# A graph layer that gathers every tile of edge rows on POOL, with no rows fetched one by one, and counts every fourth gather

## The chip, the cores and the metric

The kernel runs on one core of one Trainium2 chip. The metric is the time of one execution on the device in microseconds (us). The median of three runs of the kernel before is 1577.52 us (1574.93 to 1591.05 us).

The engines are named as the profile names them: PE is TensorE (PEld is its loading of weights), DVE is VectorE, ACT is ScalarE, POOL is GpSimd, SP is SyncE. A "q" behind a name (SPq, ACTq) means the engine's sequencer, which issues DMAs, loads registers and waits.

## The reference, cut to what matters

There are 6250 nodes with 128 features, 106250 edges sorted by destination, and 40 relation types.

```python
S   = segment_sum(x[src], dst * 40 + edge_type)          # (6250, 40, 128)
cnt = segment_sum(ones,   dst * 40 + edge_type)          # (6250, 40)
agg = einsum('nrd,rdf->nf', S, relation_weights) + cnt @ rFeatures
h   = agg * deg ** -0.5                                  # deg: edges per destination, at least 1
h   = relu(h + h @ loop_weight)
out = layernorm(x + h, axis=-1)
```

The costly part is `x[src]`: one row of 128 features for each of the 106250 edges, read in an order that the data give, and its sum into (destination, relation) cells.

## The kernel before, in words

**Tiles and blocks.** The edges are cut into 831 tiles of 128 edges (the last has 10). Seventeen tiles make a block (`TPB`), and a block of tiles belongs roughly to 128 destination nodes. There are 49 blocks; `i` is the block, `k` the place of a tile in it, and t = 17 i + k the tile.

**What a tile goes through.** (1) The 128 rows of the tile's sources are brought from DRAM into SBUF. From tile 51 on they come from `x_parts`, a copy of x in which each row is 1 KB: a high part and a low part, whose sum is the fp32 value. The first 51 tiles are gathered from x itself into `raw` and split by ACT and DVE. (2) DVE makes a one-hot matrix of 128 edges by 480 cells (`one_hot`, L896), 40 relations times a window of 12 nodes. (3) PE multiplies (L1148, two matmuls of 480 columns, one for each part) into one of six PSUM banks; a small matmul for each tile (L1130) counts the edges. (4) ACT copies 11 of the 12 window columns from PSUM to `ring` (L692) and (5) DVE adds the first column to what is there (L1028). Then the bank is free again. Between the tiles PE also multiplies the finished block before with the 40 relation weights (`relations`, L1160), and the nodes of the block before that are finished (layer norm and store).

**How rows come in.** There are three ways.

- POOL gathers a whole tile by one indirect DMA (`gather`, L572; L579 for the first 51). A gather writes `rows[:, k]`, so tile t needs tile t - 17 to be done: POOL waits for `tile_done` (L571), which PE raises by two after every odd `k` and by one after k = 16.
- The 19 tiles of `BY_ROW` (18 tiles from block 6 on, 41 tiles apart as a rule, and the last one with 10 rows) are fetched by SP, one DMA of 1 KB for each row: 18 times 128 and 10, that is 2314 DMAs. SP loads 32 row addresses into registers at a time (L523) and then issues 32 DMAs (L526). Six tiles can be held in `by_row`; before tile j SP waits until tile j - 6 of its list is done (L519).
- The 5 tiles of `BY_ACT` are fetched in the same way by ACT, one row after each copy (`fetch`, called at L694, DMA at L669): 640 DMAs.

PE waits before L1148 for the tile's own rows: `by_row_landed`, `by_act_landed` or `gathered` (L1132 to L1138).

**The count of gathers.** Each gather also raises `gather_issued` when its descriptors are written (`engine_sem`), 807 times in all. DVE waits for it before each add (L1026 and L1027): at tile t the gather of tile t + 17 - t // 4 must be issued, and from tile 48 on that of tile t + 5. Nothing else reads this count.

**Order at the start.** SP loads edges and x, issues 19 small loads of the row numbers for its list (L496 to L498), then the load of the window positions (L500), for which ACT and DVE wait, and then stores the parts of x (L476). DVE turns row numbers into byte addresses (L1051 and L1053) before its main loop. POOL gathers tiles 0 to 50 from x beside this. Gathers from `x_parts` begin when all of it is stored.

Of the kernel before, what the change touches and what calls it, by code (L numbers as in the profile page):

```python
# [14 lines left out]
P = 128  # L15
# [7 lines left out]
TPB = 17  # L23
# [15 lines left out]
ROW_LOAD = 32  # L39
# [10 lines left out]
SAFE = 6  # L50
SUMS_FROM = 10
# [20 lines left out]
ROW_TILE = 6  # L72
BY_ROW = [(6 + j * 41 // 17) * TPB + ROW_TILE for j in range(18)] + [-(-E // P) - 1]
BY_ROW_BUFS = 6
ACT_FROM = 4
ACT_ROWS = 1
ACT_BLOCKS = 8
ACT_TILE = 12
BY_ACT = [i * TPB + ACT_TILE for i in [*range(ACT_FROM + ACT_BLOCKS, BLOCKS - 1, ACT_BLOCKS)]]
ACT_BUFS = 2  # L80
ACT_LOAD = 4
ROW_BYTES = 2 * D * 4
# [23 lines left out]
assert ACT_ROWS * ACT_BLOCKS * TPB >= P and P % ACT_LOAD == 0 and BY_ACT[-1] < FULL and not set(BY_ACT) & set(BY_ROW)  # L106
# [26 lines left out]
def build(nc, x, src_main, src_by_tile, src_rest, dst_main, dst_rest, type_main, type_rest, r_features, relation_w, loop_w, out):  # L133
    with ExitStack() as ctx:
# [65 lines left out]
        by_row = x_out.rearrange("p h n c d -> p (h n) c d")  # L200
        by_act = by_row[:, BY_ROW_BUFS:BY_ROW_BUFS + ACT_BUFS]
        act_src = sb("act_src", [len(BY_ACT), P], I32)
        act_at = sb("act_at", [len(BY_ACT), P], I32)
        by_row_src = sb("by_row_src", [len(BY_ROW), P], I32)
        by_row_at = sb("by_row_at", [len(BY_ROW), P], I32)
        x_bytes = x_parts.bitcast(U8).rearrange("n b -> (n b)").unsqueeze(0)
# [82 lines left out]
        by_row_cleared = sem("by_row_cleared")  # L289
        by_row_src_loaded = sem("by_row_src_loaded")  # L290
        by_row_ready = sem("by_row_ready")
        act_src_loaded = sem("act_src_loaded")
        act_ready = sem("act_ready")
        by_act_landed = [sem(f"by_act_landed{j}") for j in range(len(BY_ACT))]
        by_row_landed = [sem(f"by_row_landed{j}") for j in range(len(BY_ROW))]
# [56 lines left out]
        def gathers_through(t):  # L352

            return t + 1 - len([n for n in BY_ROW + BY_ACT if n <= t])
# [94 lines left out]
        def _(sp):  # L449
# [6 lines left out]
            sp.dma_start(act_src[:], src_by_tile[BY_ACT[0]:BY_ACT[-1] + 1:ACT_BLOCKS * TPB, :]).then_inc(act_src_loaded, 16)  # L456
# [49 lines left out]
            def in_order():  # L506
# [6 lines left out]
                sp.wait_ge(src_loaded, 2 * 16)  # L513
                for b in range(STAGE_BUFS):
                    sp.wait_ge(staged[b], stage_count(b) * 16)
                sp.wait_ge(by_row_ready, 1)
                for j, t in enumerate(BY_ROW):
                    if j >= BY_ROW_BUFS:
                        sp.wait_ge(tile_done, BY_ROW[j - BY_ROW_BUFS] + 1)  # L519
                    for first in range(0, rows_in_tile(t), ROW_LOAD):  # L520
                        ps = range(first, min(first + ROW_LOAD, rows_in_tile(t)))
                        index = [sp.alloc_register(f"sp_row{j}_{p}") for p in ps]
                        sp.load(index, by_row_at[j:j + 1, ps[0]:ps[-1] + 1])  # L523
                        for p, reg in zip(ps, index):
# [781 lines left out]
```

## Time and profile before

| what | value |
|---|---|
| median of the runs | 1577.52 us (1574.93 to 1591.05) |
| span of the profiled execution | 1576.6 us |
| PE busy | 1049.6 us (67%) |
| DVE busy | 732.7 us (46%) |
| POOL busy | 798.1 us (51%), 756 gathers from `x_parts` and 51 from x |
| ACT busy | 528.4 us (34%) |
| DMA packets | 71124, 127.58 MB, 81 GB/s on average |
| mean granted TensorE clock | 0.853 of full speed |

The profile shows one execution, whose own time is its span of 1576.6 us, 0.9 us below the median. "Busy" leaves out what sequencers do, so SP, which only issues, has no busy time at all. Waits are listed as "engine, its line <- what ended the wait: us in total, times, longest". "issue" means that nothing in the profile explains the wait, and "remote" that a semaphore's update was seen to which no instruction's end belongs.

### The profile page before, as it was taken

Reading aid. Unit: us, or ns where it says so; the run is one execution under the profiler, and the core shown is the slowest. Engines: PE = TensorE matmul, PEld = TensorE weight load, DVE = VectorE, ACT = ScalarE, POOL = GpSimd, SP = SyncE. Lnnn points to the kernel's source line nnn. Section 1 sums busy time; section 2 is a strip of 40 time slices with the busy share of each in tenths; the row PEclk is TensorE's granted clock in tenths of the full one; section 3 lists DMA queues with packets and bytes.
Section 4 is the critical chain, followed back from the end, with each engine's and each line's share of the span. In section 5 each row is a group of like instructions: output and inputs, shape, how many; then the busy total and the mean of one; then the engine's idle time right before and its main releaser. Section 6 shows DMA issues by size and latency. Waiting matters only on the chain.

```text
span 1576.6 us, 31507 instructions
## 1 busy us (share of the span) xinstructions
PE 1049.6 (67%) x6713; PEld 931.1 (59%) x6713; DVE 732.7 (46%) x2573; ACT 528.4 (34%) x1119; POOL 798.1 (51%) x822
## 2 busy tenths in 40 slices
PE   1388777847774768474687486746576657774868
PEld 0277667736763668464576375635565546664758
DVE  5464555525452545243455254534354525552545
ACT  2353333323332334232343133323243313331433
POOL 7536565626562556353555264636364635562650
PEclk9989998969796888687998798968798979877989
DMA  6623332313231323131333132313132312231320
GB/s 200 215 62 89 90 92 77 93 45 91 77 91 46 87 78 88 48 91 44 88 87 89 45 84 70 95 46 89 54 88 70 91 51 83 82 88 46 86 77 22
DMA packets 71124, 127.58 MB, mean 81 GB/s; under 512 B 18417, under 2 KB 44002, under 8 KB 70930
## 3 DMA queue, kind: packets, MB, share of 16 engines
q0 software_dynamic: 37920, 102.48, 22.9%
q1 hardware_dynamic: 17698, 16.04, 3.3%
q10 hardware_dynamic: 15312, 7.01, 1.6%
q8 instruction: 56, 0.92, 0.3%
q14 instruction: 138, 1.13, 0.2%
HBM read 115.86 MB, written 9.60 MB: 80 GB/s over the span
## 4 chain that ended last, share of the span: by engine, by line
SPq 58%; issue 33%; PE 3%; DMA 0%; DVE 0%; ACT 0%; DVEq 0%; ACTq 0%
SPq L526 50%; SPq L523 8%; PE agg_ps L1160 1%; PE win_ps L1148 1%; PE win_ps L1233 1%; DMA x_parts<-x_out 0%; DMA x_out<-x_parts 0%; PE win_ps L1186 0%; ACT ring L692 0%; PE win_ps L1130 0%; PE win_ps L1237 0%; PE win_ps L1185 0%; DVE h_sb L935 0%; DVE y_sb L939 0%; DVE y_mid L945 0%
## 5 line engine op out<-in xcount | busy, mean ns | idle before, releaser
L572 POOL DMA_INDIRECT rows<-x_parts,src x756 | 745.8, 986 | 717.9 <-PE win_ps L1148 414.4
L692 ACT COPY ring<-win_ps 128x451 f32 x831 | 465.4, 560 | 948.5 <-PE win_ps L1148 420.1
L1160 PEld LDWEIGHTS agg_ps<-ring,w 128*128 128x128 f32 x3936 | 619.6, 210 | 106.4 <-issue 56.5
L1160 PE MATMUL agg_ps<-ring,w 128*128 128x128 f32 x3936 | 629.8, 294 | 45.0 <-issue 44.1
L1148 PE MATMUL win_ps<-hot,rows 128*128 128x480 f32 x1614 | 595.9, 457 | 12.3 <-issue 10.0
L1028 DVE TENSOR_TENSOR ring<-ring,win_ps 128x41 f32 x831 | 187.1, 225 | 808.2 <-ACT ring L692 606.2
L896 DVE TENSOR_SCALAR hot<-iota,key_f 128x480 fp32r<-128x480 f16 x831 | 393.7, 474 | 3.7 <-issue 3.7
L1148 PEld LDWEIGHTS win_ps<-hot,rows 128*128 128x128 f32 x1614 | 271.6, 210 | 14.7 <-issue 10.2
L1130 PE MATMUL win_ps<-hot_node,hot_type 128*128 128x12 bf16 x831 | 87.3, 172 | 214.9 <-DVE ring L1028 109.9
L1130 PEld LDWEIGHTS win_ps<-hot_node,hot_type 128*128 128x128 bf16 x831 | 70.9, 103 | 262.1 <-issue 215.1
L1148 PE MATMUL win_ps<-hot,x_out 128*128 128x480 f32 x48 | 24.1, 597 | 230.2 <-DMA x_out<-x_parts 227.4
L1148 PEld LDWEIGHTS win_ps<-hot,x_out 128*128 128x128 f32 x48 | 10.4, 270 | 231.8 <-DMA x_out<-x_parts 228.8
L579 POOL DMA_INDIRECT raw<-x,src x51 | 50.5, 991 | 22.6 <-issue 17.8
L916 DVE TENSOR_TENSOR hot_type<-iota,typ_f 128x320 bf16<-128x320 f16 x98 | 49.6, 506 | 0.0
L964 DVE TENSOR_TENSOR ring<-ring 128x492 f32<-128x492 f32 x48 | 31.8, 662 | 0.0
L975 DVE COPY ring<-zeros 128x492 f32<-128x492 f32 x47 | 30.8, 656 | 0.0
L990 DVE COPY ring<-zeros 128x492 f32<-128x492 f32 x47 | 30.3, 645 | 0.0
L1186 PE MATMUL win_ps<-loop,agg_sb 128*128 128x128 f32 x96 | 23.6, 323 | 3.8 <-issue 3.8
L909 DVE TENSOR_TENSOR hot_node<-iota,rel_f 128x96 bf16<-128x96 f16 x98 | 25.3, 258 | 0.4 <-issue 0.4
L1185 PEld LDWEIGHTS win_ps<-ones,cnt_sb 128*128 128x128 f32 x96 | 18.5, 194 | 3.5 <-issue 0.7
L641 ACT CAST rows<-raw 128x256 fp32r<-128x256 f32 (+1 forms) x27 | 10.4, 394 | 22.0 <-remote 18.7
L1186 PEld LDWEIGHTS win_ps<-loop,agg_sb 128*128 128x128 f32 x96 | 15.2, 197 | 4.0 <-issue 4.0
(94 smaller groups left out, 259.7 us busy)
## 6 DMA issues: line engine op xcount, KB each, us to landing
x_out<-x_parts SPq DMA_DIRECT2D x2314, 1.0 KB
rows<-x_parts,src POOLq DMA_INDIRECT x756
x_out<-x_parts ACTq DMA_DIRECT2D x640, 1.0 KB
x_parts<-x_out SPq DMA_DIRECT2D x6, 512.0 KB
x_parts<-ring SPq DMA_DIRECT2D x6, 512.0 KB
out<-out_sb ACTq DMA_DIRECT2D x48, 64.0 KB
x_blk<-x ACTq DMA_DIRECT2D x47, 64.0 KB
w<-relation_w SPq DMA_DIRECT2D x8, 320.0 KB
```

The source lines that it names most:

```text
L523: sp.load(index, by_row_at[j:j + 1, ps[0]:ps[-1] + 1])
L526: sp.dma_start(by_row[p:p + 1, j % BY_ROW_BUFS].rearrange("p c d -> p (c d)").bitcast(U8), x_bytes[:, bass.ds(at, ROW_BYTES)]).then_inc(by ...
L572: pool.indirect_dma_start(rows[0:n, k].rearrange("p c d -> p (c d)").bitcast(F32), None, x_parts, bass.IndirectOffsetOnAxis(ap=src[0:n, t: ...
L579: pool.indirect_dma_start(raw[:, t % RAW], None, x, bass.IndirectOffsetOnAxis(ap=src[:, t:t + 1], axis=0), engine_sem=gather_issued).then_ ...
L692: nc.scalar.copy(ring[:, :, bass.ds(start + 1, WIN - 1)], win_ps[bank_of(t)][:, :, 1:WIN]).then_inc(copied, 1)
L896: nc.vector.tensor_scalar(hot[:, buffer], iota[:], key_f[:, column(t)], None, ALU.is_equal).then_inc(hot_ready, 1)
L916: nc.vector.tensor_tensor(hot_type[:, at, 0:R], iota[:, 0:R].unsqueeze(1).to_broadcast([P, n, R]), typ_f[:, ts].unsqueeze(2).to_broadcast( ...
L1028: nc.vector.tensor_tensor(a, a, win_ps[bank_of(t)][:, :, 0:1], ALU.add).then_inc(added, 1)
L1130: nc.tensor.matmul(banks[bank_of(n)][:, R * WIN:COLS * WIN], hot_type[:, n % TPB], hot_node[:, n % TPB], start=True, stop=True)
L1148: ins = nc.tensor.matmul(banks[bank_of(t)][:, 0:R * WIN], of[:, part], hot[:, t % HOTS], start=False, stop=(part == PARTS - 1), skip_group ...
L1160: ins = nc.tensor.matmul(sums_of(c), w[:, r, :], ring[:, r, bass.ds(seg, BLOCK)], start=(r == 0), stop=(r == COLS - 1))
L1186: nc.tensor.matmul(ps[:, 0:D], agg_sb[:], loop[:], start=True, stop=True).then_inc(fin_done, 1)
```

## The change

The 24 tiles of `BY_ROW` and `BY_ACT` are gathered by POOL like all others, from the same `x_parts` into `rows[:, k]`. SP's and ACT's fetches go, with the loads of row numbers, the address arithmetic, and their buffers and semaphores. POOL then makes 831 gathers. Only the gathers with t % 4 == 3 raise `gather_issued` (207 times), and DVE waits for (last + 1) // 4 of them, where `last` is as before.

```diff
+SIGNAL = 4
-BY_ROW = [(6 + j * 41 // 17) * TPB + ROW_TILE for j in range(18)] + [-(-E // P) - 1]
-BY_ACT = [i * TPB + ACT_TILE for i in [*range(ACT_FROM + ACT_BLOCKS, BLOCKS - 1, ACT_BLOCKS)]]
...
         def gathers_into(k, t):
-            return len([n for n in range(k, t + 1, TPB) if n not in BY_ROW and n not in BY_ACT])
+            return len(range(k, t + 1, TPB))
...
-        def gathers_through(t):
-            return t + 1 - len([n for n in BY_ROW + BY_ACT if n <= t])
+        def signals_through(t):
+            return (t + 1) // SIGNAL
...
-            sp.dma_start(act_src[:], src_by_tile[BY_ACT[0]:BY_ACT[-1] + 1:ACT_BLOCKS * TPB, :]).then_inc(act_src_loaded, 16)
...
-            sp.wait_ge(by_row_cleared, 1)
-            for j, t in enumerate(BY_ROW):
-                of = src_by_tile[t:t + 1, :] if t < FULL else src_rest.rearrange("p o -> o p")
-                sp.dma_start(by_row_src[j:j + 1, 0:rows_in_tile(t)], of).then_inc(by_row_src_loaded, 16)
...
-                for j, t in enumerate(BY_ROW):
-                    if j >= BY_ROW_BUFS:
-                        sp.wait_ge(tile_done, BY_ROW[j - BY_ROW_BUFS] + 1)
-                    for first in range(0, rows_in_tile(t), ROW_LOAD):
-                        ...
-                            sp.dma_start(by_row[p:p + 1, j % BY_ROW_BUFS].rearrange("p c d -> p (c d)").bitcast(U8),
-                                         x_bytes[:, bass.ds(at, ROW_BYTES)]).then_inc(by_row_landed[j], 16)
...
+            def signal_of(t):
+                return gather_issued if t % SIGNAL == SIGNAL - 1 else None
             def gather(t):
-                if t in BY_ROW or t in BY_ACT:
-                    return
...
-                        bass.IndirectOffsetOnAxis(ap=src[0:n, t:t + 1], axis=0), engine_sem=gather_issued).then_inc(
+                        bass.IndirectOffsetOnAxis(ap=src[0:n, t:t + 1], axis=0), engine_sem=signal_of(t)).then_inc(
                             gathered[k], 16)
...
-                        fetch(i, k)
...
-                        dve.wait_ge(gather_issued, gathers_through(last))
+                        dve.wait_ge(gather_issued, signals_through(last))
...
-                dve.wait_ge(act_src_loaded, 16)
-                nc.vector.tensor_scalar(act_at[:], act_src[:], float(ROW_BYTES), None, ALU.mult).then_inc(act_ready, 1)
-                dve.wait_ge(by_row_src_loaded, len(BY_ROW) * 16)
-                nc.vector.tensor_scalar(by_row_at[:], by_row_src[:], float(ROW_BYTES), None, ALU.mult).then_inc(by_row_ready, 1)
...
-                    if t in BY_ROW:
-                        pe.wait_ge(by_row_landed[BY_ROW.index(t)], rows_in_tile(t) * 16)
-                    elif t in BY_ACT:
-                        pe.wait_ge(by_act_landed[BY_ACT.index(t)], P * 16)
-                    else:
-                        pe.wait_ge(gathered[k], gathers_into(k, t) * 16)
+                    pe.wait_ge(gathered[k], gathers_into(k, t) * 16)
...
-                if t in BY_ROW:
-                    of = by_row[:, BY_ROW.index(t) % BY_ROW_BUFS]
-                elif t in BY_ACT:
-                    of = by_act[:, BY_ACT.index(t) % ACT_BUFS]
-                else:
-                    of = rows[:, k]
+                of = rows[:, k]
```

## Rows read from the trace of the kernel before

**Rows 1.** The page's chain that ended last, by engine.

```profile
SPq 58%; issue 33%; PE 3%; DMA 0%; DVE 0%; ACT 0%; DVEq 0%; ACTq 0%
```

**Rows 2.** All waits of the span: us in total, times, longest us.

```profile
POOL rows L572 <- PE win_ps L1148: 414.4, 114, 23.5
...
PE win_ps L1148 <- DMA x_out<-x_parts: 227.4, 15, 22.4
...
POOL rows L572 <- remote: 108.7, 46, 2.8
...
DVE ring L1028 <- DMA rows<-x_parts,src: 48.8, 38, 4.8
```

**Rows 3.** Line L526, SP's row DMAs: ns min/median/max, first and last start.

```profile
L526 SPq DMA_DIRECT2D x_out<-x_parts x2314: 3/224/772, 90.7 to 1526.1; - x193
```

**Rows 4.** SP in two windows: start, length, instructions merged.

```profile
1416.38 24.61 SPq L526 DMA_DIRECT2D x_out<-x_parts  x57
...
1466.21 11.14 SPq L526 DMA_DIRECT2D x_out<-x_parts  x17
```

**Rows 5.** Three stretches: length, busy us (x instructions) by engine, clock, DMA.

```profile
0.00:97.00 97.00, 37.07 (x163) 25.89 (x164) 54.56 (x165) 34.95 (x74) 52.34 (x66) 0.96 0.56 176
97.00:1538.20 1441.20, 979.92 (x6285) 873.94 (x6285) 659.16 (x2331) 480.45 (x1011) 744.82 (x756) 0.84 0.27 76
1538.20:1576.60 38.40, 32.56 (x269) 31.27 (x267) 18.99 (x78) 12.97 (x35) 0.94 (x1) 0.95 0.08 22
```

**Rows 6.** Line L572, POOL's gathers from x_parts.

```profile
L572 POOL DMA_INDIRECT rows<-x_parts,src x756: 943/949/1387, 97.0 to 1538.2; - x189
```

**Rows 7.** POOL in order of time, one burst: start, us, [idle before <- releaser].

```profile
1467.88 0.95 POOL L572 DMA_INDIRECT rows<-x_parts,src  x1 [1.91 <-remote]
...
1474.22 0.95 POOL L572 DMA_INDIRECT rows<-x_parts,src  x1 [0.30 <-issue]
1477.38 0.95 POOL L572 DMA_INDIRECT rows<-x_parts,src  x1 [2.22 <-remote]
```

**Rows 8.** ACT in the same window.

```profile
1470.96 0.54 ACT L692 COPY ring<-win_ps 128x451 f32 x1 [0.17 <-ACT ring L692]
1476.73 0.54 ACT L692 COPY ring<-win_ps 128x451 f32 x1 [5.24 <-remote]
```

**Rows 9.** PE in the same window.

```profile
1469.95 0.69 PE L1148 MATMUL win_ps<-hot,rows 128*128 128x480 f32 x2
```

**Rows 10.** POOL after SP's last row DMA.

```profile
1534.24 0.95 POOL L572 DMA_INDIRECT rows<-x_parts,src  x1 [0.31 <-issue]
1536.95 0.94 POOL L572 DMA_INDIRECT rows<-x_parts,src  x1 [1.76 <-PE win_ps L1148]
```

**Rows 11.** ACT at the same time.

```profile
1532.00 0.58 ACT L692 COPY ring<-win_ps 128x451 f32 x1 [0.17 <-DVE y_sum L942]
1536.30 0.58 ACT L692 COPY ring<-win_ps 128x451 f32 x1 [3.72 <-PE win_ps L1148]
```

**Rows 12.** Three stretches in which PE waits for no row fetched singly.

```profile
124.30:317.60 193.30, 148.80 (x959) 132.43 (x959) 100.29 (x357) 73.92 (x155) 115.19 (x118) 0.89 0.31 88
1447.10:1516.60 69.50, 52.37 (x349) 46.45 (x347) 37.41 (x135) 26.79 (x56) 43.96 (x44) 0.94 0.32 91
...
1538.00:1556.00 18.00, 18.00 (x141) 17.09 (x140) 11.81 (x48) 10.80 (x24) 0.94 (x1) 1.00 0.09 24
```

**Rows 13.** Line L692 in the last of these stretches.

```profile
L692 ACT COPY ring<-win_ps x18: 535/576/596, 1537.8 to 1555.1; 128x451 f32 x18
```

**Rows 14.** Line L669, ACT's row DMAs.

```profile
L669 ACTq DMA_DIRECT2D x_out<-x_parts x640: 3/240/757, 149.2 to 1397.1; - x160
```

**Rows 15.** SP at the start.

```profile
17.09 21.21 SPq L498 DMA_DIRECT2D by_row_src<-src_by_tile  x18
...
41.10 0.73 SPq L500 DMA_DIRECT2D pos<-w  x1
```

**Rows 16.** ACT at the start, its first copy.

```profile
39.85 0.54 ACT L692 COPY ring<-win_ps 128x451 f32 x1
```

More of the change, by code:

```diff
@@ L38 @@
 POS_LOAD = 4
-ROW_LOAD = 32
 ROUND_SHIFT = 10
@@ L105 @@
 assert 8 * (STAGE_BUFS - X_BUFS) <= 2 * COLS and 2 * D <= 2 * SEG
-assert ACT_ROWS * ACT_BLOCKS * TPB >= P and P % ACT_LOAD == 0 and BY_ACT[-1] < FULL and not set(BY_ACT) & set(BY_ROW)
 assert USED > LAST * TPB + SUMS_FROM and R % W_LOAD == 0 and FREE_W % W_LOAD == 0
@@ L130, in bank_of, with build @@
     return BANK_OF["tile", t]
-def build(nc, x, src_main, src_by_tile, src_rest, dst_main, dst_rest, type_main, type_rest, r_features, relation_w, loop_w, out):
+def build(nc, x, src_main, src_rest, dst_main, dst_rest, type_main, type_rest, r_features, relation_w, loop_w, out):
     with ExitStack() as ctx:
@@ L199, in build @@
         x_out = sb("x_out", [P, 2, STAGE, PARTS, D], F32R)
[L200 to L206, printed above, removed]
         hot = sb("hot", [P, HOTS, R * WIN], F32R)
@@ L288, in build @@
         gather_issued = sem("gather_issued")
[L289 to L295, printed above, removed]
         gathered = [sem(f"gathered{k}") for k in range(TPB)]
@@ L512, in in_order @@
                         w_load((n - 3) * W_LOAD)
[L513 to L516, printed above, removed]
-                for j, t in enumerate(BY_ROW):
-                    if j >= BY_ROW_BUFS:
-                        sp.wait_ge(tile_done, BY_ROW[j - BY_ROW_BUFS] + 1)
-                    for first in range(0, rows_in_tile(t), ROW_LOAD):
[L521 to L524, printed above, removed]
-                            at = sp.snap(reg, donate=True)
-                            sp.dma_start(by_row[p:p + 1, j % BY_ROW_BUFS].rearrange("p c d -> p (c d)").bitcast(U8),
-                                         x_bytes[:, bass.ds(at, ROW_BYTES)]).then_inc(by_row_landed[j], 16)
-                        for reg in index:
-                            sp.free_register(reg)
             def g_load(t):
@@ L646, in _ @@
             regs = [act.alloc_register(f"act_pos{k}") for k in range(TPB)]
-            index = []
-            def fetch(i, k):
-                j, part = divmod(i - ACT_FROM, ACT_BLOCKS)
-                if j < 0 or j >= len(BY_ACT):
-                    return
-                first = (part * TPB + k) * ACT_ROWS
-                if first == 0:
-                    if j == 0:
-                        act.wait_ge(act_ready, 1)
-                        for b in range(STAGE_BUFS):
-                            act.wait_ge(staged[b], stage_count(b) * 16)
-                    if j >= ACT_BUFS:
-                        act.wait_ge(tile_done, BY_ACT[j - ACT_BUFS] + 1)
-                for p in range(first, min(first + ACT_ROWS, P)):
-                    if p % ACT_LOAD == 0:
-                        while index:
-                            act.free_register(index.pop())
-                        index.extend(act.alloc_register(f"act_row{j}_{p + n}") for n in range(ACT_LOAD))
-                        act.load(list(index), act_at[j:j + 1, p:p + ACT_LOAD])
-                    at = act.snap(index[p % ACT_LOAD], donate=True)
-                    act.dma_start(by_act[p:p + 1, j % ACT_BUFS].rearrange("p c d -> p (c d)").bitcast(U8),
-                                  x_bytes[:, bass.ds(at, ROW_BYTES)]).then_inc(by_act_landed[j], 16)
             def step(i, tiles, sums, late, fin):
@@ L822, in stage_low_part @@
                 nc.vector.tensor_tensor(low_part, of, high_part.bitcast(F32), ALU.subtract).then_inc(stage_low, 1)
-            nc.vector.memset(by_row_src[:], 0).then_inc(by_row_cleared, 1)
             nc.vector.memset(zeros[:], 0.0).then_inc(zeros_done, 1)
```

13 lines of the change are left out of this document (1 added, 12 removed).

## The prediction

> **What bounds the kernel now.** I read the chain that ended last first: 58% of it is SP's queue [rows 1], and that is the engine which computes nothing. So the question is what waits for SP. The list of waits answers: PE stood for 227.4 us, in 15 waits of up to 22.4 us, before a matmul whose rows come from `x_out`, the buffer of the rows fetched one by one [rows 2]. In those waits nothing else moves: the 414.4 us in which POOL waits for PE are partly the same time [rows 2].
>
> Is this SP's pace or a late start? The line of its DMAs gives it: 2314 DMAs between 90.7 and 1526.1 us [rows 3], so 1435.4 / 2313 = 0.621 us each and 128 x 0.621 = 79.4 us for a tile. Tiles of this kind stand 41 apart, and 79.4 / 41 = 1.94 us for a tile of the whole kernel. Against it, the middle of the kernel (first to last gather from `x_parts`) takes 1441.2 us for 755 gaps between gathers [rows 5], 1.91 us each. SP is the bound, and it was never idle.
>
> The two windows on SP show something more [rows 4]. While all others stand (1416 to 1441) it issues 57 DMAs in 24.61 us, 0.43 each. While POOL gathers (1466 to 1477) it issues 17 in 11.14 us, 0.66 each. A burst of gathers slows other sequencers, and it does so to ACT's and POOL's waits as well. The matmul of 1469.95 us [rows 9] is that of tile 778 (I count by the semaphores of its gathers), and its end releases ACT's copy of tile 777. That copy starts at 1476.73 after 5.24 us idle [rows 8], though PE had the tile done near 1470.6. POOL was in a burst of six gathers from 1467.88, whose last began at 1474.22 and ended at 1475.17; it resumed at 1477.38 [rows 7]. I read it so: while gathers follow each other without a gap, the updates of PE's semaphore are seen late, and come about 1.4 us after the burst. Such a cycle is 1477.38 - 1467.88 = 9.50 us for six gathers, 1.58 us for one. I call this the hold. It is inferred, not shown; it is what will be left when SP's wait is gone.
>
> **The change, part by part.**
>
> (a) *SP's rows go.* PE's 227.4 us go whole [rows 2]: they are waits of the engine that everything else waits for, and SP issues nothing else at that time that is needed. What is late next is not the gather: POOL spends 414.4 us waiting for PE [rows 2], so it stands 17 tiles ahead, at the end of its buffers.
>
> (b) *POOL gathers 24 tiles more.* A gather back to back takes 0.949 us and a gap of 0.30 [rows 6, 7], 1.25 us; in the hold cycle it costs 1.58. So 24 cost 30 to 38 us if POOL's bursts set the pace, and nothing if PE does. I take 38.
>
> (c) *ACT's 640 fetches go.* One costs ACT's sequencer 0.240 us as a median [rows 14]. What it does to the pace I read from stretches without a wait for single rows: 193.3 / 118 = 1.64 us for a gather while ACT fetches, and 69.5 / 44 = 1.58 after its last fetch at 1397 us [rows 12, 14]. That is 0.06 us x 779 = 47 us, with nothing as the lower end, since the stretches are short. The waits of (a) hid part of this already: after a long wait all buffers are full.
>
> (d) *The start.* SP's 19 small loads sit from 17.1 us to the load of the positions at 41.1 [rows 15], and ACT's first copy begins at 39.85 [rows 16]. Without them it can start earlier, but the 51 gathers from x run beside it, in one burst. I take 4 us, since that burst stays; the ends are 0 and 21, the length of the small loads.
>
> (e) *The count of every fourth gather.* It is raised 207 times instead of 807, and DVE asks for a gather up to three earlier than before, so its wait ends no later. DVE's waits that ended with a gather are 48.8 us in 38 [rows 2], and I give none of it back, since POOL is 17 tiles ahead where DVE asks for 5. Whether a gather without the count is shorter no row shows, as every gather has it. The bound is the gap of 0.30 us behind each [rows 7]: 779 x 3/4 x 0.30 = 175 us less, or nothing. A gain of zero is nearest to what I can support: the gap could as well be the descriptors' own.
>
> *The sum.* After the first gather from `x_parts` there are 780 gathers, so 779 gaps. First part 97.0 - 4 = 93; middle 779 x 1.58 = 1231; last part 38.4 as now [rows 5]. Together 1362 us. The other way round, 1576.6 - 227.4 + 38 - 4 = 1383, which leaves (c) out. I forecast 1365 us. The profiled execution is 0.9 us below the median of the runs, so no correction is made.
>
> *A rule of the Trainium skill beside it.* In the late stretch DVE was busy for 37.41 of 69.50 us [rows 12], and over the span the gathers' median stayed at their minimum, 949 against 943 ns [rows 6]. Advanced Engine Details and Errata (VectorE Performance Modes) says that GpSimd's instructions and two-port vector instructions block each other on a shared SBUF port, which speaks against more work on POOL. By that rule gathers would lengthen beside a busier DVE, where the median shows none of it; the slow rival below has the same place, with a price from rows.
>
> **The rivals.**
>
> *The hold eases.* Perhaps the row DMAs of SP and ACT are part of what makes updates late. Then the pace falls from 1.58 towards POOL's back-to-back 1.25: 93 + 779 x 1.25 + 38 = 1105 us, half way 1233. PE would allow it: with no gathers in the way it does 18 tiles in 18.0 us at full clock [rows 12, 13]. Against it: after SP's last DMA (1526.1) a burst that ended at 1535.19 still left ACT idle for 3.72 us, until 1536.30 [rows 10, 11]. Chance 0.16.
>
> *The count was dear.* Three of four gaps of 0.30 go: 1362 - 175 = 1187 us. For it: POOL's gap is as regular as a fixed handshake. Against: nothing shows what is in it. Chance 0.14.
>
> *No relief, and the catching-up is lost.* The pace stays at the 1.64 of the long stretch: 93 + 1278 + 38 = 1409 us. Chance 0.07.
>
> *Slower.* POOL's gathers get longer beside a DVE that no longer pauses. Place: L572 itself. Price: from 949 to its maximum of 1387 ns [rows 6], 0.438 us more, 1362 + 341 = 1703 us. It decides from (1576.6 - 1362) / 779 = 0.276 us more, a mean of 1.22 us for a gather. Against it is the median at the minimum. Chance 0.06, a third of it within 1% of now.
>
> *Half of the change does nothing.* That is my forecast for (e); rows fetched one by one cannot stay, as their DMAs are gone from the program.
>
> **How the numbers follow.** My forecast, 1325 to 1405, has 0.57. With the third rival the stretch up to 1430 holds some 0.62. To leave out no more than 0.2 the range must reach down over the count (1187) and over most of the way of an easing hold (1233): 1180 to 1430. All cases but the slow one are faster by over 1% (the least that a measurement of this kernel tells from no change): 0.94. Within 1%: 0.02. Slower: 0.04.
>
> **What would show it.** Right: no wait of PE for `x_out`; 831 gathers, the median still 949 ns and 0.30 us apart; POOL in bursts of about six with 2 us between; POOL's start-to-start mean over the middle at 1.58; ACT's waits marked "remote" or for PE of 3 to 5 us behind the bursts; ACT's first copy before 39.85 us. The pace is the number to look at first: 1.25 means that the hold has eased, and a gap under 0.30 that the count was in it. Wrong on the slow side: gathers above 1.2 us, or DVE's add waiting for a gather. If PE's longest waits are still over 10 us, something else than SP's rows set them.

## The result, and the profile after the change

Measured beside the kernel before on one chip, the changed kernel took 1361.58 us as the median of 4 runs (1357.35 to 1365.42), the kernel before 1582.24 us (1574.93 to 1591.05, 4 runs): ratio 0.8596, 95% interval 0.8555 to 0.8638. The forecast was 1365 us.

That is not the whole result. The experiments were run on five more occasions, B to F, each on another chip, with the kernel before beside them each time. The number of chip A isn't on record, so A may be one of D, E or F. The chips are of two kinds (4 runs or more where no number stands):

| Chip | Kernel before, median us | Kernel run beside it | median us | Ratio (95%) |
|---|---|---|---|---|
| A (the forecast's) | 1582.24 | the changed kernel | 1361.58 | 0.860 (0.856 to 0.864) |
| B | 1051.95 | changed, count by each gather | 1076.86 | 1.023 (1.021 to 1.025) |
| B | | before, SP's rows to POOL | 1071.25 | 1.018 (1.016 to 1.020) |
| B | | before, ACT's rows to POOL | 1056.09 | 1.004 (1.003 to 1.005) |
| B | | changed, no gathers from tile 102 on | 946.3 (1 run) | |
| C | 1052.37 | **the changed kernel** | **1113.70** | **1.058 (1.057 to 1.060)** |
| C | | changed, no gathers from tile 102 on | 947.97 (2 runs) | 0.901 (0.899 to 0.903) |
| D | 1583.87 | before, count by every fourth | 1579.95 | 0.998 (0.995 to 1.002) |
| D | | changed, no count, DVE doesn't wait | 1355.69 | 0.857 (0.853 to 0.862) |
| D | | before, ten tiles by ACT, not five | 1484.65 | 0.937 (0.932 to 0.941) |
| E | 1578.09 (1 run) | four stretches | 1236.39 (1 run) | |
| F | 1579.2 | changed, pause behind every 5th gather | 1359.11 (2 runs) | 0.860 (0.853 to 0.867) |
| F | | changed, short pause behind every 3rd | 1363.33 (2 runs) | 0.863 (0.855 to 0.871) |

The same program is 14% faster on one chip and 5.8% slower on another. What I called the hold is there on A, D, E and F and not on B and C, and the kernel before takes 1580 us with it and 1052 without. The granted TensorE clock differs too, 0.91 of full speed on A and 0.99 on C as the mean of the changed kernel's profile. It doesn't account for the difference in time: PE is busy for 1064 us on A and 978 on C, 86 us more, where the span is 249 us longer. Every run listed here was recorded by the profiler, so none shows whether the recording has a part in it.

**The profile on chip A.** The page, rows of the chain, the gathers, ACT's copy and DVE's add:

```profile
span 1360.0 us, 25380 instructions
...
PE 2%; DVE 0%; ACT 0%; issue 0%; DVEq 0%; ACTq 0%
...
L525 POOL DMA_INDIRECT rows<-x_parts,src x780 | 769.1, 986 | 476.9 <-issue 200.9
L620 ACT COPY ring<-win_ps 128x451 f32 x831 | 466.1, 561 | 751.5 <-remote 477.6
...
L954 DVE TENSOR_TENSOR ring<-ring,win_ps 128x41 f32 x831 | 186.1, 224 | 620.8 <-ACT ring L620 513.3
```

SP's 58% of [rows 1] is gone from the chain, which breaks off after 2% and so says nothing of the middle. The waits say more:

```profile
engine line waited for: us in total, times, longest us
DVE ring L954 <- ACT ring L620: 513.3, 174, 8.9
ACT ring L620 <- remote: 477.6, 101, 14.1
POOL rows L525 <- issue: 200.9, 638, 4.4
ACT ring L620 <- PE win_ps L1060: 156.8, 91, 6.2
POOL rows L525 <- PE win_ps L1060: 146.7, 78, 24.5
POOL rows L525 <- remote: 129.3, 64, 2.7
```

PE's wait for `x_out` of [rows 2] has no successor, and POOL's wait for PE fell from 414.4 to 146.7 us. ACT's copy is what waits. The windows that answer to [rows 5], cut at the first and last gather from `x_parts`:

```profile
core 0: us, PE busy (x) PEld busy (x) DVE busy (x) ACT busy (x) POOL busy (x), PEclk, DMA share, GB/s
0.00:101.78 101.78, 39.20 (x163) 27.01 (x164) 53.24 (x162) 34.72 (x74) 53.36 (x66) 0.97 0.54 168
101.78:1322.39 1220.61, 994.12 (x6300) 875.77 (x6300) 646.41 (x2337) 477.02 (x1013) 768.23 (x779) 0.90 0.31 90
1322.39:1360.00 37.61, 30.79 (x253) 29.45 (x251) 17.03 (x72) 11.66 (x32) 0.88 (x1) 0.95 0.07 20
```

The pace is 1220.61 / 779 = 1.567 us a gather (forecast 1.58). A burst on POOL and ACT's copies beside it, the rows that answer to [rows 7, 8]; columns are start, duration, instruction, idle time before it:

```profile
701.11 0.94 POOL L525 DMA_INDIRECT rows<-x_parts,src  x1 [2.07 <-remote]
...
710.35 0.99 POOL L525 DMA_INDIRECT rows<-x_parts,src  x1 [0.30 <-issue]
713.48 0.94 POOL L525 DMA_INDIRECT rows<-x_parts,src  x1 [2.14 <-remote]
```

```profile
704.63 0.54 ACT L620 COPY ring<-win_ps 128x451 f32 x1
708.47 0.57 ACT L620 COPY ring<-win_ps 128x451 f32 x1 [3.30 <-PE win_ps L1060]
709.21 0.58 ACT L620 COPY ring<-win_ps 128x451 f32 x1 [0.17 <-issue]
712.85 0.58 ACT L620 COPY ring<-win_ps 128x451 f32 x1 [3.06 <-remote]
```

Eight gathers from 701.11, the last ending at 711.34; the copy comes at 712.85, 1.5 us later, after 3.06 us idle. In the whole trace, counted one by one, there are 125 bursts (a burst ends where POOL is idle for over 0.5 us), most of 5 to 8 gathers (before: 166, many of two), and 133 copies that stood over 2 us, 605 us in all.

**What is late in the hold.** The trace also keeps when each semaphore was raised. On C, and in the same way on B, PE's `tile_done` is raised 12 to 15 ns behind the end of its matmul in the middle of the kernel, every time, so the modelled ends can be trusted. On A, between the first and the last gather from `x_parts`, 257 of 414 updates come over 0.5 us behind it. ACT isn't slow to see them: 131 of the 133 copies start within 0.12 us of an update. So what is late is the update itself, and when it is late depends on the place in POOL's burst:

| PE's matmul ended while POOL was in | matmuls | updates over 0.5 us late |
|---|---|---|
| the first or second gather of a burst | 108 | 25 |
| the third | 63 | 44 |
| the fourth or a later one | 182 | 176 |
| a pause of over 0.5 us | 61 | 12 |

### The profile page after: what moved, and what is told of

Read it like the earlier page. It is cut to its first block and busy times, and to the rows that moved or that the text cites. A ratio compares the mean times of both kernels' runs of the same rounds, so it can differ in the third digit from the quotient of the medians.

```text
span 1360.0 us, 25380 instructions
## 1 busy us (share of the span) xinstructions
PE 1064.1 (78%) x6713; PEld 932.2 (69%) x6713; DVE 716.7 (53%) x2570; ACT 523.4 (38%) x1119; POOL 822.5 (60%) x846
## 5 line engine op out<-in xcount | busy, mean ns | idle before, releaser
L525 POOL DMA_INDIRECT rows<-x_parts,src x780 | 769.1, 986 | 476.9 <-issue 200.9
L1072 PE MATMUL agg_ps<-ring,w 128*128 128x128 f32 x3936 | 640.7, 293 | 104.9 <-issue 102.8
L1060 PE MATMUL win_ps<-hot,rows 128*128 128x480 f32 x1662 | 617.8, 457 | 44.0 <-issue 42.6
L822 DVE TENSOR_SCALAR hot<-iota,key_f 128x480 fp32r<-128x480 f16 x831 | 393.7, 474 | 1.9 <-issue 1.9
L1060 PEld LDWEIGHTS win_ps<-hot,rows 128*128 128x128 f32 x1662 | 281.1, 209 | 65.5 <-issue 61.8
L1052 PEld LDWEIGHTS win_ps<-hot_node,hot_type 128*128 128x128 bf16 x831 | 75.9, 104 | 165.9 <-issue 103.8
L842 DVE TENSOR_TENSOR hot_type<-iota,typ_f 128x320 bf16<-128x320 f16 x98 | 49.7, 508 | 0.0
L890 DVE TENSOR_TENSOR ring<-ring 128x492 f32<-128x492 f32 x48 | 31.9, 664 | 0.0
L901 DVE COPY ring<-zeros 128x492 f32<-128x492 f32 x47 | 30.7, 654 | 0.0
L916 DVE COPY ring<-zeros 128x492 f32<-128x492 f32 x47 | 30.3, 644 | 0.0
L1097 PEld LDWEIGHTS win_ps<-ones,cnt_sb 128*128 128x128 f32 x96 | 22.3, 233 | 3.9
L662 ACT COPY fin_sb<-win_ps 128x129 f32<-128x129 f32 x48 | 13.0, 271 | 25.9 <-remote 24.0
L871 DVE TENSOR_SCALAR y_mid<-y_sb,y_sum 128x128 f32<-128x128 f32 x49 | 16.4, 335 | 0.1
L1097 PE MATMUL win_ps<-ones,cnt_sb 128*128 128x1 f32 x96 | 15.4, 230 | 0.0
```

The source lines that it names most:

```text
L525: pool.indirect_dma_start(rows[0:n, k].rearrange("p c d -> p (c d)").bitcast(F32), None, x_parts, bass.IndirectOffsetOnAxis(ap=src[0:n, t: ...
L822: nc.vector.tensor_scalar(hot[:, buffer], iota[:], key_f[:, column(t)], None, ALU.is_equal).then_inc(hot_ready, 1)
L842: nc.vector.tensor_tensor(hot_type[:, at, 0:R], iota[:, 0:R].unsqueeze(1).to_broadcast([P, n, R]), typ_f[:, ts].unsqueeze(2).to_broadcast( ...
L890: nc.vector.tensor_tensor(ring[:, :, bass.ds(head, WIN)], ring[:, :, bass.ds(head, WIN)], ring[:, :, bass.ds(tail + BLOCK, WIN)], ALU.add) ...
L1052: nc.tensor.matmul(banks[bank_of(n)][:, R * WIN:COLS * WIN], hot_type[:, n % TPB], hot_node[:, n % TPB], start=True, stop=True)
L1060: ins = nc.tensor.matmul(banks[bank_of(t)][:, 0:R * WIN], of[:, part], hot[:, t % HOTS], start=False, stop=(part == PARTS - 1), skip_group ...
```

## The experiments

**1. The four runs on chip B.** They met the other kind of chip, so each expectation is read for what it says of its mechanism; the times in it are those of the chips with the hold. First the count:

```
-SIGNAL = 4
+SIGNAL = 1
```

> The changed kernel with the count raised by every gather again (SIGNAL = 1), all else as changed. My theory: the count costs nothing in either place, so 1362 us, within 1355 to 1370, the gap behind a gather 0.30 us and the burst of about six as before. Rival (the count was dear, or its updates add to what ACT waits for): the gap grows or the pace of a gather rises from 1.57 us; by the bound of the prediction up to 175 us more, 1537 us. A third, that DVE's wait ends later with the coarser count, would make this kernel faster, by at most the 49 us that DVE waited for gathers in the kernel before.

1076.86 us. Chip C then gave the changed kernel itself:

> The changed kernel itself, beside the kernel before on one more chip. The first four runs met a chip on which the kernel before takes 1052 us: no hold, POOL's gathers unbroken at 1.25 us. The change then has another sign there. If this chip has no hold: POOL's queue is the bound and gets 24 gathers more, 24 x 1.254 = 30 us at most; the kernel with the count by each gather took 1076.9, so 1077 us if the coarser count gives nothing, ratio 1.023. If this chip has the hold (the kernel before near 1580 us): 1362 us, ratio 0.86, as first measured. Rival: the hold comes and goes between programs and not between chips, then the two kernels of this call can differ in it, and the ratio can be anything from 0.68 to 1.3.

1113.70 us: with the kernel before equal on both chips (1051.95 and 1052.37), the coarse count costs 36.8 us there, the opposite of the rival that called the count dear. (The two counts never ran on one chip; that they compare rests on the kernel before and on the profiles that follow.) The gathers of the two profiles, fine count and coarse count:

```profile
L525 POOL DMA_INDIRECT rows<-x_parts,src x780 | 740.3, 949 | 237.6 <-issue 158.7 <-PE win_ps L1060 78.9
```

```profile
L525 POOL DMA_INDIRECT rows<-x_parts,src x780 | 775.6, 994 | 237.7 <-issue 176.7 <-PE win_ps L1060 60.9
```

The idle time between gathers is the same to 0.1 us. The gathers themselves are longer, by 35.3 us in all, and as POOL has no other gap from the first gather from `x_parts` to the last, that is nearly all of the 36.8 us. No version here is shown to beat both kernels on both kinds of chip; other than the two kernels, each full version met one kind alone. The reason for the longer gathers stands in the timeline of DVE and POOL. Coarse count:

```profile
502.30 0.46 DVE L822 TENSOR_SCALAR hot<-iota,key_f 128x480 fp32r<-128x480 f16 x1
503.00 0.50 DVE L822 TENSOR_SCALAR hot<-iota,key_f 128x480 fp32r<-128x480 f16 x1
503.42 0.51 DVE L842 TENSOR_TENSOR hot_type<-iota,typ_f 128x360 bf16<-128x360 f16 x1
506.22 0.23 DVE L954 TENSOR_TENSOR ring<-ring,win_ps 128x41 f32 x1 [2.29 <-DMA rows<-x_parts,src]
...
507.40 0.65 DVE L890 TENSOR_TENSOR ring<-ring 128x492 f32<-128x492 f32 x1
```

```profile
503.57 1.18 POOL L525 DMA_INDIRECT rows<-x_parts,src  x1 [0.30 <-PE win_ps L1060]
505.05 0.94 POOL L525 DMA_INDIRECT rows<-x_parts,src  x1 [0.30 <-issue]
506.30 0.95 POOL L525 DMA_INDIRECT rows<-x_parts,src  x1 [0.31 <-issue]
507.55 1.32 POOL L525 DMA_INDIRECT rows<-x_parts,src  x1 [0.30 <-issue]
```

The gather of 503.57 starts while DVE is in L842 until 503.93 and takes 1.18 us; that of 507.55 meets L890, which ends at 508.05, and takes 1.32. Each is longer than 0.946 by what was left of DVE's instruction at its start, less 0.13 us. At 505.05 DVE is idle: 0.94. Fine count:

```profile
503.90 0.23 DVE L954 TENSOR_TENSOR ring<-ring,win_ps 128x41 f32 x1 [0.46 <-DMA rows<-x_parts,src]
504.04 0.46 DVE L822 TENSOR_SCALAR hot<-iota,key_f 128x480 fp32r<-128x480 f16 x1
505.15 0.23 DVE L954 TENSOR_TENSOR ring<-ring,win_ps 128x41 f32 x1 [0.66 <-ACT ring L620]
505.29 0.46 DVE L822 TENSOR_SCALAR hot<-iota,key_f 128x480 fp32r<-128x480 f16 x1
```

```profile
503.98 0.95 POOL L525 DMA_INDIRECT rows<-x_parts,src  x1 [0.30 <-PE win_ps L1060]
505.23 0.95 POOL L525 DMA_INDIRECT rows<-x_parts,src  x1 [0.30 <-issue]
```

DVE's add waits for the count, so it starts 0.22 us behind a gather's end, and the large instruction behind it (504.04) starts 0.06 us after the next gather has started (503.98), which is not lengthened by it. Counted over both traces: of the 182 gathers of 1.0 us or more under the coarse count, 180 found DVE busy 0.1 us before their start, of the 598 shorter ones 234. Under the fine count only 17 are that long, and of 763 short ones 67 found DVE busy. The time over 0.946 us a gather sums to 37.7 against 2.4 us. The kind of instruction counts, not its length: of the gathers under the coarse count that start over 0.18 us before the end of DVE's instruction, 78 of 104 take 1.0 us or more in L822 and all 42 do in L842 and L890, but none of 23 does in the copies of `zeros` at L901 and L916, though such a copy takes 0.65 us. DVE isn't held up in turn: 726 one-hots that start 0.03 to 0.12 us behind a gather's start under the fine count take 0.46 us as a median and 0.47 at most.

So the count is no bookkeeping: by these traces DVE's wait for it keeps DVE's large instructions out of the moment in which a gather starts. The run that takes the wait out altogether met a chip with the hold (experiment 4), so on a chip without it the mechanism rests on these counts. Advanced Engine Details and Errata (VectorE Performance Modes) of the Trainium skill says that GpSimd and two-port vector instructions block each other. These traces agree in part: some of DVE's instructions block a gather that starts in them. They don't tell which of them use two ports, and they show no lengthening of a gather that is already on its way.

**2. Only the rows back to POOL, on B.** The kernel before with one of these edits, each with its loads of indices:

```
-BY_ROW = [(6 + j * 41 // 17) * TPB + ROW_TILE for j in range(18)] + [-(-E // P) - 1]
+BY_ROW = []
```

```
-BY_ACT = [i * TPB + ACT_TILE for i in [*range(ACT_FROM + ACT_BLOCKS, BLOCKS - 1, ACT_BLOCKS)]]
+BY_ACT = []
```

> The kernel before, with only SP's rows given to POOL (19 tiles; SP's 19 small loads of indices go with them); ACT still fetches its five tiles row by row, and the count is raised by every gather. My theory: SP's pace is the whole bound, and ACT's fetches cost 0.06 us for each gather: 1362 + 0 to 47, I say 1385 us, PE without a wait for x_out over 5 us. Rival (ACT's rows cost nothing): 1355 to 1365 us. Rival (the wait moves to ACT's own rows, 128 in eight blocks, 24 us late as SP's were): over 1420 us.

> The kernel before, with only ACT's rows given to POOL (5 tiles); SP still fetches its 19 tiles row by row and the count is raised by every gather. My theory: SP's queue stays the bound, 2314 DMAs at 0.62 us; nothing of the 216 us is gained: 1560 to 1582 us. Rival (ACT's fetches beside the gathers slow SP too, 0.43 us alone against 0.66 beside): SP's DMAs get faster, down to 0.55 us each, and the time falls to about 1420 us.

1071.25 us (19.3 more than before) and 1056.09 (4.1 more). On this chip POOL is the bound, with all its gathers in one unbroken chain 1.254 us apart, and a tile given to it costs less than that: 19.3 us for 19 tiles, 4.1 for 5, 24.9 for all 24 (1076.86 against 1051.95). What the two expectations say of a chip with the hold stays untested. SP keeps up here. In the second kernel its row fetches run so:

```profile
L525 SPq DMA_DIRECT2D x_out<-x_parts x2314: 224/225/327, 65.2 to 978.1; - x193
```

912.9 / 2313 = 0.395 us each, against 0.621 on A [rows 3]. At 41 tiles x 1.254 = 51.4 us between two such tiles, 128 x 0.395 = 50.5 us is just in time. The median distance between two fetches is 0.32 us on both chips, but on A one in six is over 1 us. Split by what POOL does, the mean on A is 0.87 us while it gathers and 0.36 while it stands: the hold slows SP's queue too. The fetches row by row are a gain on a chip of this kind and a loss on A's.

**3. No gathers, on B and C.** The changed kernel with STOP = 102, and the counts that are waited for cut to match:

```
-                for t in range(TPB, USED):
+                for t in range(TPB, STOP):
```

> The changed kernel without the gathers from tile 102 on: rows keeps what the last gathers left, so this part of the sums is not the reference's; PE, ACT and DVE do all their work, and no gather is in their way. My theory of the hold (while gathers follow each other, PE's updates are seen late, and PE then stands with its six banks full): the pace of a tile falls from 1.57 us to 1.0 to 1.15, so 102 tiles as now (some 145 us) and 729 x 1.0 to 1.15: 900 to 1020 us in all, and ACT's waits over 2 us are gone. Rival (the engines' own hand-over through six banks sets 1.57, and gathers are hidden under it): 1300 to 1362 us. If DVE's work or PE's clock sets it: about 1.25 to 1.4 us a tile, 1100 to 1200 us.

> The changed kernel without the gathers from tile 102 on (its sums are not the reference's), beside the changed kernel on one chip. If this chip has the hold: by my theory (it comes from the gathers) 102 tiles at the held pace and 729 at the engines' own, which was 1.07 us on the chip without the hold (18.2 us a block): 927 to 990 us. Rival (on that chip PE's updates are late for a reason that has nothing to do with the gathers): over 1200 us. If it has none: 946 us again.

946.3 and 947.97 us; a block of 17 tiles takes 18.2 us, 1.07 a tile. In the window from 139 to 903 us PE is busy for 763.91 of 764.00 us: without gathers PE is the bound.

**4. The parts of (e) on a chip with the hold, D.** The kernel before, with a count raised by `gathers_through(t) % SIGNAL == 0` alone:

```
-                        dve.wait_ge(gather_issued, gathers_through(last))
+                        dve.wait_ge(gather_issued, gathers_through(last) // SIGNAL)
```

> The kernel before with one part of the change alone: the count of gathers is raised at every fourth only, rows are fetched as before. On a chip without the hold (the kernel before near 1052 us). My theory now: DVE's add waits for the count, so with a count by each gather DVE starts 0.2 us behind a gather's end and has its instructions done when the next gather wants to start; with a count by every fourth it no longer does, a gather that finds DVE busy at its start waits, and the mean gather grows from 0.949 to 0.99 us: 755 x 0.045 = 34 us more, 1086 us. Rival (the coarse count only made DVE wait longer, and with less to gather it does not matter): 1052 to 1058 us with the mean gather at 0.950. On a chip with the hold (near 1580): the mean gather is 0.986 already and SP is the bound, so 1575 to 1590 us.

And the changed kernel, where no gather raises the count:

```
-                        dve.wait_ge(gather_issued, signals_through(last))
```

> The changed kernel without the count of gathers at all, and DVE's add without its wait for it. My theory (a gather that finds DVE busy at its start is longer, and only DVE's wait kept the two apart), on a chip without the hold: DVE runs free, as with the coarse count or worse, mean gather 0.99 to 1.03 us, 1110 to 1145 us against 1077 with a count by each gather. Rival (the count itself, or DVE's late release by the coarse one, is what costs 37 us): without it the gather is 0.949 again and POOL sets 1077 us or a little less. On a chip with the hold: 1362 us like the changed kernel by my theory of the hold, since DVE's wait was never late there.

1579.95 us (0.998, same) and 1355.69 us (0.857, the changed kernel's 0.860 within the intervals). The mean gather is 986 ns in the first and 984 in the second, as it was before and after the change. With the hold DVE isn't in step with POOL anyway, and the count does nothing, so the 14% on A come from the rows alone. What the two expectations say of a chip without the hold stays untested.

**5. More tiles by ACT, on D.** The kernel before with

```
-ACT_ROWS = 1
-ACT_BLOCKS = 8
+ACT_ROWS = 2
+ACT_BLOCKS = 4
```

> The kernel before with ten tiles fetched row by row by ACT, two rows behind each copy, instead of five with one. Without the hold POOL's queue is the bound at 1.254 us for a gather; five gathers fewer save up to 6.3 us, of which the five that are there saved 4.1 (1056.1 against 1052.0): 1046 to 1050 us. Rival (ACT's fetches, 0.24 us each and twice as many behind each copy, hold up the adds and so DVE's places between gathers): no gain or 1052 to 1065 us. On a chip with the hold: SP stays the bound, 1575 to 1600 us.

Missed: 1484.65 us, 6.3% less. SP's fetches now run from 93.0 to 1430.8 us, 0.578 us each where the kernel before has 0.621, and 76 copies stood over 2 us (280 us in all) where the kernel of experiment 4 on the same chip has 133 (603 us). POOL makes 221 bursts where that kernel has 170, so they are shorter, and 54% of PE's updates are over 0.5 us late against 66%. Why SP gets faster with more fetches beside it I can't say; only that its pace isn't a constant of the chip.

**6. Four stretches in one kernel, on E.** Without SP's rows; ACT fetches in blocks 4 to 11; then gathers alone; then

```
+                    if t >= PAUSE_FROM and t % 3 == 2:
+                        nc.gpsimd.memset(x_out[:, 0].bitcast(F32).rearrange("p n c d -> p (n c d)"), 0.0).then_inc(paused, 1)
+                        pool.wait_ge(paused, (t - PAUSE_FROM) // 3 + 1)
```

then no gathers.

> The kernel before without SP's rows, in four stretches that are read apart: blocks 4 to 11 with ACT's fetches of one tile beside the gathers; 12 to 23 with gathers alone; 24 to 33 with a memset of 128x1024 (1 to 2 us) on POOL behind every third gather; from block 34 on no gathers (rows keeps old values, so the sums there are not the reference's). Read by the time of a block of 17 tiles. On a chip with the hold, by my theory (PE's updates are seen only once POOL's gathers pause): 27.9 us a block, then 26.6, then copies that come behind each memset's start in threes, 17/3 x (3 x 1.25 + about 1.8) = 31 us a block, and 18.2 us without gathers. Rival (that chip's updates are late, whatever POOL does): 26 us or more in the last stretch too. Rival (any wait of POOL, not the end of the gathers' data, lets the updates through): the third stretch is as above, but copies start at once with the memset and not 1.4 us behind. On a chip without the hold: 21.3, 21.3, 31 (POOL's own length alone, copies in no groups of three) and 18.2 us.

The windows of the four stretches, cut at ACT's first copy of blocks 4, 12, 25, 34 and 48 (block 24, which still used up the lead, is left out):

```profile
core 0: us, PE busy (x) PEld busy (x) DVE busy (x) ACT busy (x) POOL busy (x), PEclk, DMA share, GB/s
149.51:367.25 217.74, 172.26 (x1108) 151.35 (x1107) 115.92 (x408) 83.33 (x176) 131.78 (x136) 0.91 0.31 88
367.25:683.36 316.11, 258.37 (x1647) 227.74 (x1646) 170.37 (x613) 124.28 (x264) 199.80 (x203) 0.90 0.31 89
702.03:942.72 240.69, 191.69 (x1222) 163.71 (x1221) 155.68 (x461) 93.00 (x198) 190.56 (x197) 0.96 0.31 87
942.72:1197.14 254.42, 254.42 (x1919) 236.78 (x1918) 196.32 (x715) 144.09 (x308) 0.00 (x0) 1.00 0.03 9
```

Divided by 136, 204, 153 and 238 tiles: 1.601, 1.550, 1.573 and 1.069 us. The last number settles one thing: on a chip with the hold, the hold goes when the gathers go, and what is left is the 1.07 us of chips B and C, so nothing is slow there but what stands beside gathers. All 126 updates of PE in that stretch are again raised within 15 ns of its matmuls' ends. The third stretch did not do what I expected (31 us a block; it is 26.7). I had counted 1.8 us for a pause; POOL's cycle of three is

```profile
767.38 0.95 POOL L572 DMA_INDIRECT rows<-x_parts,src  x1 [0.27 <-POOL x_out L592]
768.63 0.95 POOL L572 DMA_INDIRECT rows<-x_parts,src  x1 [0.30 <-issue]
769.89 0.95 POOL L572 DMA_INDIRECT rows<-x_parts,src  x1 [0.30 <-issue]
770.83 0.97 POOL L592 MEMSET x_out<- 128x1024 f32 x1
772.07 0.95 POOL L572 DMA_INDIRECT rows<-x_parts,src  x1 [0.27 <-POOL x_out L592]
```

4.69 us, 1.563 a tile: POOL itself was the bound, and its own length with these pauses happens to be the pace that it has with the hold. So this stretch could show no gain in time. It does show the updates: 11 of 81 came over 0.5 us late, where the stretch before it, with as many gathers in a us but in longer bursts, has 68 of 108. Copies that stood over 2 us fell from 31 (142 us, 204 tiles) to 15 (42 us, 153 tiles).

Copies did not start in threes with each memset. The longest stand of ACT, 4.02 us until 782.29, had another cause, though:

```profile
779.71 1.56 DVE L959 TENSOR_SCALAR out_sb<-y_mid,rstd 128x128 f32<-128x128 f32 x1
...
781.30 0.35 ACTq L732 DMA_DIRECT2D out<-out_sb  x1
782.29 0.54 ACT L695 COPY ring<-win_ps 128x451 f32 x1 [4.02 <-issue]
```

ACT's queue waited to store `out_sb`, which DVE finished at 781.27. That instruction takes 0.28 us as a median and 1.56 here, with POOL's memset (780.22 to 781.19) beside it. The memset is no empty pause; it also holds up DVE.

**7. Fewer or shorter pauses, on F.** These would beat both kernels on such a chip if each pause let the updates through and cost nothing else. The changed kernel with `SIGNAL = 1` and, with EVERY, PAUSE = 5, 1024 or 3, 256,

```
+                    if t >= PLAIN and t % EVERY == EVERY - 1:
+                        nc.gpsimd.memset(x_out[:, 0].bitcast(F32).rearrange("p n c d -> p (n c d)")[:, 0:PAUSE], 0.0).then_inc(
+                            paused, 1)
+                        pool.wait_ge(paused, (t + 1) // EVERY - PLAIN // EVERY)
```

> The changed kernel with the count by each gather and a memset of 128x1024 on POOL (0.97 us, 1.24 between two gathers) behind every fifth gather from x_parts. On a chip with the hold: if each pause of 1.24 us lets PE's updates through, POOL's own length is left, (5 x 1.254 + 0.94) / 5 = 1.44 us a gather: 102 + 779 x 1.44 + 38 = 1262 us, which beats both kernels there. Rival (the release needs the 1.4 to 1.6 us that stood behind each burst): many pauses pass unused, and it is 1362 us or up to 1480. On a chip without the hold the pauses are pure loss: 1077 + 156 x 0.94 = 1224 us.

> The same with a memset of 128x256 (some 0.35 us, 0.6 between two gathers) behind every third gather. On a chip with the hold: if a pause of 0.6 us is enough, (3 x 1.254 + 0.3) / 3 = 1.35 us a gather, 1193 us. If it is too short, the hold stays as it is without pauses: 1362 to 1400 us, in bursts of six gathers and more. On a chip without the hold: 1077 + 260 x 0.3 = 1155 us.

1359.11 and 1363.33 us, the changed kernel's time again. The memsets (156 of 970 ns, 260 of 385) only took the place of idle time: POOL stood 324.6 and 367.1 us before its gathers, where the changed kernel has 476.9. POOL's rows in the first of the two, and DVE's one-hots:

```profile
L527 POOL DMA_INDIRECT rows<-x_parts,src x780 | 769.6, 987 | 324.6 <-issue 189.2 <-PE win_ps L1066 76.2 <-remote 43.2
L547 POOL MEMSET x_out<- 128x1024 f32 x156 | 151.4, 970 | 0.0
...
L828 DVE TENSOR_SCALAR hot<-iota,key_f 128x480 fp32r<-128x480 f16 x831 | 506.3, 610 | 0.8 <-issue 0.7
```

From first to last gather the pace is 1218.63 / 779 = 1.564 and 1222.08 / 779 = 1.569 us, against 1.567. Held copies were more and shorter, 150 with 544 us and 157 with 570 us, against 133 with 605. Of PE's updates 67% and 68% were over 0.5 us late, against 62%.

This doesn't show that pauses do nothing. Each kernel has a flaw as a test. In the first, 90 pauses of 1.24 us found an update outstanding, and 52 of them let one through; but the memsets held up DVE, whose one-hots took 506 us in place of 394. In the second the one-hots took 419 us, but the pauses of 0.6 us were too short: of 67 that found an update outstanding, 2 let one through. So the pauses of 1.24 us let through a good half, and the pace of 1.57 us stayed. A pause that leaves DVE alone has not been run.

## Why the prediction was right, and what in it was wrong

**What bounds the kernel** was right for chip A: PE's wait for SP's rows was what cost it. The wait is gone there, and experiment 4 leaves only the rows as the cause. In the first stretch on E, which differs from the kernel before in SP's rows, a tile takes 1.60 us, where the same blocks of the kernel before take 1.75 on A. It was wrong as a statement on the kernel. On B and C the same program isn't bound by SP at all. The 0.43 us for a fetch alone [rows 4] was the hint that I had and did not follow: at that pace SP nearly keeps up (55 us for 51), and SP's distance of 0.87 us beside gathers is part of the hold.

**(a), (b)** fit: PE's wait for `x_out` is gone, and the span is 216.6 us shorter. 38 us for the 24 gathers is the pace times 24, 1.567 x 24; no run on a chip with the hold isolates it.

**(c)** ACT's fetches were put at 0.06 us a gather. On E the stretches with and without them differ by 1.601 - 1.550 = 0.05, 40 us for 47. They follow each other in one run and single blocks there range from 22.7 to 31.2 us, so this is a size and no proof. Experiment 5 speaks against it: with twice as many fetches by ACT the kernel before got 99 us faster.

**(d) failed: the gain is not there.** Taken: 4 us sooner. Measured: the first gather from `x_parts` at 101.78 us, not 97.0. In the five kernels without SP's loads on a chip with the hold it comes between 97.9 and 101.8, and in the three with them at 96.4, 97.0 and 99.6, so a small loss is more likely than a gain. ACT's first copy did come sooner, at 24.76 against 39.85 [rows 16], but the first block then took 55.9 us against 36.9. The burst of 51 gathers from x ended in both (its last began at 76.3, and at 74.5 before), and the copies stood beside it in the hold. On C, without the hold, that burst ends alike (71.7), the first block takes 23.0 us and the first gather from `x_parts` comes at 73.14. The cover was named (the burst stays), and the earlier start was credited all the same.

**(e)** was right on the chips with the hold and wrong without it: plus 36.8 us. The step that failed is the sentence that DVE "asks for a gather up to three earlier than before, so its wait ends no later". A wait that ends earlier was taken as harmless. It also sets when DVE's next large instructions run, and POOL pays for those that meet a gather's start.

The sign of it stood on the page of the kernel before. The prediction read the median of 949 ns, but the mean there is 986:

```profile
L572 POOL DMA_INDIRECT rows<-x_parts,src x756 | 745.8, 986 | 717.9 <-PE win_ps L1148 414.4
```

151 of the 756 gathers took 1.0 us or more, 30.6 us over 0.946 in all. With the hold POOL has time to spare and this costs nothing; without it each of them counts.

**The sum** was worked out as 93 + 1231 + 38.4 = 1362.4 us and measured as 101.8 + 1220.6 + 37.6 = 1360.0: off by +8.8, -10.4 and -0.8 us. Two errors cancel, so the small difference says little on how good the terms are.

**The hold** is there, and its consequence (1.57 to 1.58 us a gather) was right. The mechanism as put, that updates are late while gathers follow each other and come about 1.4 us after the burst, fits the trace: on A 97% of PE's updates are late from the fourth gather of a burst on, and with a pause behind every third gather on E only 14% are. What failed is the step from there in experiment 7, that a pause of 1.24 us would always let them through and leave POOL's own length: it was 1.564 us a gather, not 1.44. What else the runs show: the hold needs gathers (1.07 us without); it needs neither the count nor DVE's wait nor rows fetched one by one; it slows SP's queue as well; ACT's own updates reach DVE within 0.13 us in nine of ten of the add's waits in the same trace; and the gathers' data isn't late, with the last packet 2.42 us behind a gather's start on A and 2.43 on C (medians). What delays PE's updates, and why on one kind of chip alone, stays open.

**The rivals.** *The hold eases*: not by this change. *The count was dear*: no; the gap is 0.30 us with it and without it. *Slower*: its place was the right one, gathers beside DVE, and what happens on C agrees in its direction with the Trainium skill's rule from Advanced Engine Details and Errata (VectorE Performance Modes), by which two-port vector instructions and GpSimd's block each other. Its price was not: a mean of 0.994 us on C, where I had said that it decides from 1.22. That threshold was worked out from a kernel bound by SP. Where POOL is the bound from the start, it decides from nothing, and 24 more gathers alone turn the sign (1.023). The range of 1180 to 1430 us holds A's time and not C's 1113.70, and the 0.94 for faster was a chance for chips like A.

## What to carry to other kernels

A wait between two engines may be there for its timing and not for its data: before you loosen one, look at what the released engine does next and whose instruction it meets. Read the mean beside the median: where they differ, some of the instructions pay for something. In a profile with gaps that nothing explains, work out what the kernel would be bound by without them; if that is another engine, the change can have the other sign on another chip, so measure on more than one. A pause made by an instruction is not empty: look at what it does to the other engines before you conclude from it. And look for the shortest spacing of a queue that seems to be the bound: if it is a third below the mean, the queue is slowed by something, and removing its work treats the symptom.

## What the runs showed of the hardware that I had not expected

- One program, the kernel before, takes 1052 us on B and C and 1580 on A, D, E and F, the runs of a kind within 2% of each other.
- On A an update of PE's semaphore is late by 0.5 us or more for 97% of the matmuls that end in the fourth or a later gather of a burst, and for 23% in the first two; on C it comes 12 to 14 ns behind every matmul, in one unbroken chain of 780 gathers.
- Row fetches on SP's queue follow each other at 0.87 us on A while POOL gathers, at 0.36 there while it stands, and at 0.395 on B, where it always gathers (means); the DMA instruction itself takes 224 ns as a median on both.
- A gather of 128 rows of 1 KB costs POOL 0.946 to 0.952 us as a median and 0.30 behind it in every kernel and on every chip. One that starts in certain of DVE's instructions (L822, L842, L890) is longer by what is left of that instruction less 0.13 us as a median on C: 1.18 and 1.32 us in the rows shown. One that starts in a copy of the same length (L901, L916) isn't.
- A memset of 128x1024 on POOL holds up DVE: one instruction of 0.28 us took 1.56 beside it, and with 156 of them the mean one-hot is 610 ns for 474.
- On a chip with the hold the changed kernel's pace is 1.567 us with POOL free, and 1.564 and 1.569 with 156 pauses of 0.97 us and 260 of 0.39.
